# Selective scan stage: one activation table for Exp and Ln, the gate's Silu in four blocks between the last copies, first convolution products from two turned blocks

## The reference, cut to what matters

```
xz = x @ W_in;  xs, z = split(xz)
A = -(1..16)                                  # same for every channel
xs = silu(conv4(xs, conv_x_w) + conv_x_b)     # u
z  = silu(conv4(z, conv_z_w) + conv_z_b)      # the gate
dt_low, B, C = split(xs @ W_xdbl)             # 64, 16, 16
delta = softplus(dt_low @ W_dt + 2 * inv_dt)
for each token, for each state n of 16:
    h[n] = exp(-(n+1) * delta) * h[n] + delta * u * B[n]
    y += h[n] * C[n]
y = y + u * D
x = layernorm(x + concat(y, z) @ W_out + b_out)
```

## Time and profile before

| | us |
|---|---|
| median of 3 executions | 2578.47 |
| lowest, highest | 2573.18, 2580.49 |
| the profiled execution: its time | 2579.75 |
| its span (first to last instruction in the trace) | 2578.0 |
| the stage in question, from its first product to the last layer norm statistics | about 566.5 to 736 |
| PE, DVE, ACT, POOL busy over the whole span | 93%, 78%, 58%, 47% |

### The profile page before, as it was taken

The page is one execution under the profiler, slowest core; times in us unless marked ns, Lnnn a source line. Parts: engine busy times, 40 slices in busy tenths (PEclk is TensorE's granted clock), DMA queues, the critical chain, the costliest instruction groups (busy, mean ns, idle before and its releaser), DMA issues.

```text
span 2578.0 us, 41400 instructions
## 1 busy us (share of the span) xinstructions
PE 2385.0 (93%) x15006; PEld 1114.8 (43%) x15006; DVE 2009.2 (78%) x3088; ACT 1485.4 (58%) x2648; POOL 1202.6 (47%) x985
## 2 busy tenths in 40 slices
PE   6799997998969977997899999999999999999898
PEld 4444445452346754774333334333343334333345
DVE  7798886428979947875688897989888897989742
ACT  5586664637559946983555554555545554555462
POOL 2211112305847733762256665666656665666730
PEclk9799998999989999998999999999999999999999
DMA  5000001010000000000100000000000000000000
GB/s 218 1 1 1 1 1 59 1 70 1 0 17 2 2 1 1 2 2 17 46 5 10 10 6 9 10 10 6 9 9 10 10 6 9 10 10 9 6 1 17
DMA packets 21431, 39.37 MB, mean 15 GB/s; under 512 B 10542, under 2 KB 12718, under 8 KB 20332
## 3 DMA queue, kind: packets, MB, share of 16 engines
q1 hardware_dynamic: 21228, 36.73, 4.1%
HBM read 32.80 MB, written 2.35 MB: 14 GB/s over the span
## 4 chain that ended last, share of the span: by engine, by line
PE 76%; DVE 14%; ACT 4%; issue 4%; POOL 1%; DMA 0%; DVEq 0%; ACTq 0%; POOLq 0%; SPq 0%
PE PS L2978 16%; PE PS L2969 16%; PE PS L1393 6%; PE PS L2941 5%; PE PS L2151 2%; PE PS L2200 2%; PE PS L1375 2%; PE PS L814 2%; PE PS L815 2%; PE PS L816 2%; DVE NR L3189 1%; PE PS L2220 1%; PE PS L2924 1%; DVE WK L1925 1%; PE PS L2216 1%
## 5 line engine op out<-in xcount | busy, mean ns | idle before, releaser
L3088 ACT ACTIVATE WK<-PS 128x1024 f32<-128x1024 f32 x512 | 497.2, 1022 | 457.5 <-PE PS L2969 454.5
L3268 POOL TENSOR_TENSOR W<-W,WK 128x512 f32<-128x512 f32 x448 | 574.9, 1284 | 387.0 <-DVE W L3207 387.0
L3189 DVE TENSOR_REDUCE NR<-PS 128x2 f32<-128x1024 f32 x512 | 625.0, 1223 | 133.9 <-PE PS L2942 117.3
L2978 PE MATMUL PS<-WK,W 128*64 128x512 f32 x2048 | 494.1, 603 | 0.0
L2969 PE MATMUL PS<-WK 64*128 64x512 f16 (+1 forms) x4096 | 484.0, 376 | 0.6 <-issue 0.6
L3207 DVE TENSOR_TENSOR W<-W,WK 128x512 f32<-128x512 f32 x448 | 338.9, 759 | 9.1 <-ACT WK L3088 9.1
L2969 PEld LDWEIGHTS PS<-WK 64*128 64x128 f16 (+1 forms) x4096 | 199.0, 94 | 220.0 <-ACT WK L3088 6.5
L2978 PEld LDWEIGHTS PS<-WK,W 128*64 128x64 f32 x2048 | 124.0, 136 | 247.5 <-issue 170.0
L2941 PE MATMUL PS<-WK 64*128 64x512 f16 x512 | 195.4, 382 | 4.0 <-DVE NR L3189 3.5
L2942 PE MATMUL PS<-WK 64*128 64x512 f16 x512 | 195.4, 382 | 0.0
L2439 POOL TENSOR_TENSOR WK<-WK 128x768 f32<-128x768 f32 (+1 forms) x64 | 147.4, 2322 | 101.8 <-DVE WK L2364 101.8
(11 more groups left out here) (379 smaller groups left out, 4365.4 us busy)
## 6 DMA issues: line engine op xcount, KB each, us to landing
XB<-l_rdens SPq DMA_DIRECT2D x62, 128.0 KB, 2.9
W<-in_mw SPq DMA_DIRECT2D x8, 512.0 KB, 12.0
W<-in_l2w SPq DMA_DIRECT2D x1, 3114.0 KB, 11.6
W<-in_f1w SPq DMA_DIRECT2D x1, 2816.0 KB, 19.1
W<-in_l3w SPq DMA_DIRECT2D x1, 2816.0 KB, 9.9
W<-in_f3w SPq DMA_DIRECT2D x1, 2816.0 KB, 9.8
W<-in_mw SPq DMA_DIRECT2D x8, 256.0 KB, 12.4
W<-W SPq DMA_DIRECT2D x4, 384.0 KB, 3.7
```

The source lines that it names most:

```text
L2978: m = e.matmul(k.PS[64 * i:64 * i + 64, 4, :], self.V[:, kt, g, :], self.PTB[kt // 2 % 2][:, kt % 2, i, :], start=kt == 0, stop=kt == NT - 1)
L3088: e.activation(self.PTB[kt // 2 % 2][:, kt % 2, :, :], self.k.PS[:, 2 * (kt % 2):2 * (kt % 2) + 2, :], ACT.Exp, scale=1.0 / 64).then_inc(s ...
L3189: e.tensor_reduce(self.PM[ji % 2][:, u // 4, :, u % 4], self.k.PS[:, bk:bk + 2, :], AX.X, ALU.max).then_inc(self.maxes.sem)
L3268: e.tensor_tensor(ac, ac, p, ALU.add).then_inc(self.acc1.sem)
```

## The change

- **Table sets.** ACT loads LOGS by hand ahead of the first Abs, and once more ahead of the loop. Exp is now done by blocks of 512 (`dexp` counts four), so the start runs Abs, Exp, Ln of block 0 and then of block 1, and unit 10 does two Exps.
- **The gate's Silu** (`act_silu`, a block of 512 each) stands ahead of each of the last four `copy_c` (units 30 and 31); `zs` counts four. `pe_out` waits for its own block, and writes to banks 7, 1, 2, 3 (`YBANK`) instead of 0 to 3.
- **Output products of block 0** move into the loop, in unit 31 between the two `rows_c`.
- **End of DVE**: layer norm of block 0, then `dve_y` of blocks 2 and 3, then the other three.
- **Start of PE**: the convolution of block 0 waits for turned blocks 0 and 1 only, that of block 1 for 0 to 2. On DVE the copy of block 0 goes between the inverses of the norm and the scaling of the last rows.
- **DVE** does `delta` and `delta_u` of block 0, then of block 1.

```
@@ LayerNorm @@
     def dve_scale(self, e):
+        self.dve_inverses(e)
+        self.dve_scale_last(e)
+
+    def dve_inverses(self, e):
...
-        self.dve_rows(e, 4 * a, NT)
+
+    def dve_scale_last(self, e):
+        self.dve_rows(e, 4 * self.early, NT)
@@ Mamba.pe @@
         self.xt.pe(e)
+        e.wait_ge(*self.folded(2))
+        self.xt.ready(e, 1)
+        self.pe_conv(e, 0)
+        self.xt.ready(e, 2)
+        self.pe_conv(e, 1)
         self.xt.ready(e, 3)
-        e.wait_ge(*self.folded(2))
-        self.pe_conv(e, 0)
-        self.pe_conv(e, 1)
...
             self.rows_c(e, u, 0)
+            if u == 31:
+                e.wait_ge(*self.ld.wout(16))
+                self.pe_out(e, 0)
...
-        e.wait_ge(*self.ld.wout(16))
-        e.wait_ge(*self.zs(1))
-        self.pe_out(e, 0)
         self.pe_out(e, 1)
@@ Mamba.pe_out @@
         e.wait_ge(*self.y(b + 1))
-        if b < 2:
-            e.wait_ge(*self.inp(63 + b))
-        else:
+        e.wait_ge(*self.zs(b + 1))
+        if b == 1:
+            e.wait_ge(*self.inp(64))
+        elif b > 1:
             e.wait_ge(*self.scan(32))
@@ Mamba.act @@
-        self.act_abs(e, 0)
-        self.act_abs(e, 1)
-        self.act_exp(e, 0)
-        self.act_ln(e, 0)
-        self.act_ln(e, 1)
+        e.preload_act_table_set(LOGS)
+        for b in range(2):
+            self.act_abs(e, b)
+            self.act_exp(e, b)
+            self.act_ln(e, b)
...
         self.act_u(e, 3)
+        e.preload_act_table_set(LOGS)
         for u in range(self.UNITS):
+            if u >= 30:
+                self.act_silu(e, 2 * u - 60)
             self.copy_c(e, u, 0)
+            if u >= 30:
+                self.act_silu(e, 2 * u - 59)
             self.copy_c(e, u, 1)
...
-                self.act_exp(e, 1)
+                self.act_exp(e, 2)
+                self.act_exp(e, 3)
...
-        e.wait_ge(*self.zraw(4))
-        e.activation(self.ZS, self.ZS, ACT.Silu, bias=c("czb")).then_inc(self.zs.sem)
         e.preload_act_table_set(LOGS)
@@ new @@
+    def act_silu(self, e, b):
+        s_ = slice(b * 512, (b + 1) * 512)
+        e.wait_ge(*self.zraw(b + 1))
+        e.activation(self.ZS[:, s_], self.ZS[:, s_], ACT.Silu, bias=self.k.c("czb")).then_inc(self.zs.sem)
@@ Mamba.dve @@
-        self.before.dve_scale(e)
+        self.before.dve_inverses(e)
         self.begin.wait(e)
-        self.xt.dve(e)
+        self.xt.dve_block(e, 0)
+        self.before.dve_scale_last(e)
+        self.xt.dve_block(e, 2)
...
         for b in range(2):
             self.delta(e, b)
-        for b in range(2):
             self.delta_u(e, b)
...
         for b in range(NB):
-            if b == 2:
+            e.wait_ge(*self.out(b + 1))
+            self.ln.dve(e, b, four(PS[:, self.YBANK[b], :]))
+            if not b:
                 self.dve_y(e, 2)
                 self.dve_y(e, 3)
-            e.wait_ge(*self.out(b + 1))
-            self.ln.dve(e, b, four(PS[:, b, :]))
```

19 lines of the change are left out of this document (10 added, 9 removed).

## The result

The changed kernel takes 2568.59 us (median of 19 runs, 2564.57 to 2574.74), the kernel before on the same chip 2580.49 us (19 runs, 2572.88 to 2586.00); the ratio is 0.9961 with a 95% interval of 0.9949 to 0.9973, so the change saves 0.4%, clear of noise. In a second series the changed kernel took 0.9953 of the time (0.9935 to 0.9971). The forecast was 2568.8 us. The profiled execution took 2564.57 us (span 2562.8, mean granted clock 0.974), that of before 2579.75.

What follows compares the result with a forecast made beforehand. DVE paces the steady loop, so the saving comes from its idle places: 0.6 (start through unit 3) + 3.2 (units 12 to 16) + 5.9 (end) = 9.7 us, from 2578.47 to 2568.8 us; range 2564.0 to 2574.5.

Steps and rivals of the forecast that it cites:

- Start: Up to the first scan: PE's rows of B are the bound; gain 1.0 us, of which 0.3 from ACT.
- Unit 3: DVE's stall for a row of B at unit 3: gain between 0.1 and 2.0 us, taken 0.6.
- Units 12 to 16: Both DVE stalls go without the two loads, POOL is late next: 15.8 us instead of 18.92, gain taken 3.2.
- three units of 0.2 + 2.5 + 1.26 = 4.0 each: POOL in units 12 to 16: its time per unit with the added delta work, putting the last delta_u at 14.8 to 14.9.
- End: After the last scan: early Silu and load, output products in the loop and norms filling DVE's wait gain 5.9 us.
- less than 0.2: Unit 31: ACT's last copy ends at 720.0, POOL is busy until 720.2, so the work put into the loop costs nothing.
- Rival 1: End gives less, PE at the lower clock during block 0's products: gain there 4.4, total 8.2, 2570.3 us; chance 0.16.
- The drain: About 1380 ns with every switch of set; would make the end's gain about 4.7 and the whole 8.5 us.
- Rivals 2: Middle stays bound by POOL and PE's order, only 1.57 goes: gain 8.1, 2570.4 us; chance 0.16 alone or with Rival 1.
- rival 3: Slower: PE's clock does not come back after its wait for the first copy of C; 2587.4 us; chance 0.03.
- a clock under 0.9 past unit 4: Sign that would show the forecast wrong: granted PE clock below 0.9 after unit 4.
- The later stages: Behind the changed stage: their being longer than before was a sign of being wrong, which no term foresaw.

Runs made afterwards that it cites:

- u4_silu_behind: Changed kernel with block 0's output products behind the loop and the four Silus with their load behind the last copies of C; last scan to last add 15.83 us against 11.67.
- m1_out0_twice: Changed kernel with the eight output products of block 0 done twice in the loop; last scan to last add 13.46 us against 11.67.

## Why the prediction was right, and where it was not

The forecast of the time held nearly to the tenth, but not by its own sum: two errors cancelled. The stage gave 11.93 and not 9.7, and the median of before, 2578.47 in three runs, is 2580.49 in nineteen. With the right base and my sum it would have been 2570.8, with my base and the right sum 2566.5; with both, 2580.49 - 11.93, it is 2568.56. That this meets the measured 2568.59 so closely is chance as well: 11.93 comes from one execution of each kernel, and the changed kernel's second profile has the stage 3.46 longer.

**Start.** Forecast 1.0, measured 1.21. The mechanism is as told: DVE ready first, PE's rows of B the bound. The first product of the convolution came 0.89 earlier instead of 0.7. With the start undone 0.98 are lost, with the tables undone 0.57; they sum to more than 1.21 because each alone leaves the other as the bound (0.64 and 0.23 are what one alone gives against before).

**Unit 3.** Taken 0.6, range 0.1 to 2.0, measured 2.16: the most mis-sized term, and above its own range because the first scan gave 1.21 and not 1.0. The step that failed is "PE, at the lower clock twice as slow ... ends the first add_up at 597.0, a row and the second add_up at 599.1". In the frame of before, the clock was back at 597.0 (595.00 + 1.97), and the second pair took 1.03. I took the length of the low spell from the row of before, where it was 6.8 us, as if the length were a property of the place. The runs show two lengths, and at this place a restart of PE 0.5 to 1 us later goes with the longer one. The prices at the low clock were also a little small: "an add_up 1.7, a row of C 0.4", where the rows have 1.91 and 0.61. "With the clock back early it is DVE's own pace" was the right branch, and I put my value near the other.

**Units 12 to 16.** Forecast 15.8, bound by POOL; measured 15.05, DVE's pace. The step that failed is the sum of POOL's unit: "three units of 0.2 + 2.5 + 1.26 = 4.0 each". They stand 3.80 apart, because consecutive rows overlap by some 0.04, three times a unit, and the 4.0 is rounded up from 3.96; and POOL's first delta began 1.23 behind scan 12, not 1.5. (The gain "taken 3.2" is also 0.1 over the text's own 18.92 - 15.8.) The last delta_u ended 13.88 behind scan 12 instead of 14.8, in time for DVE. That POOL is next stands: in the runs with the longer low spell at unit 3, or a further one behind it, scan 12 to scan 16 took 15.13 to 15.55, and in u4_silu_behind the row of DVE's wait names POOL.

**End.** Forecast 5.9, measured 5.91, and the order of events is the one foreseen. By runs, the Silus' place is 3.72, DVE's order 0.52, the products' place 0.44; the remaining 1.2 is in no single undoing, since the run with Silus and products both put back still has Silus by blocks and DVE's new order. The margin of "less than 0.2" in front of POOL was real: eight more products made POOL wait 1.65. But POOL is not what bounds the end; m1_out0_twice shows PE busy without a break and the end later by just what PE has more to do, where the text asked only who waits for the copy. Rival 1 (low clock in the loop's last units) did not come in any of the profiles with the Silus in the loop; PE's waits for copies shortly before were not twice 1.2 but once 0.81 (row 706.94 of the changed kernel's trace).

**The drain** that the Trainium skill (ScalarE: Activation LUTs, "What ACT_TABLE_LOAD costs") adds to every switch of set would, by the prediction's estimate, have made the end 4.7: the load at 704.39 ends at 705.67 and Silu starts at 705.68, and the end gave 5.91. The measurement decides against it here.

**Rivals 2 and 3** did not occur. But rival 3's mechanism, a wait of PE from which the clock takes long to return, is what made the difference at unit 3 between 2.2 and 0; it cost one to two microseconds there and not eighteen. The prediction named a clock under 0.9 past unit 4 as a sign of being wrong. It occurs (0.66 in 611 to 616, behind PE's wait of 2.42 for DVE in unit 5) and costs nothing: DVE has no wait behind it, and before has the same 0.66 in 616 to 621. The later stages, on which I had put a condition, are 1.28 shorter in the profile after, with the same kernel text; over the 14 profiles the part behind the last add varies by 4 us.

## What to carry to other kernels

Where PE stands idle in a stage that another engine paces, ask for the time at which it resumes and not only for how long it waits: here a microsecond there came back as two at the next place where that engine is late. A chain that you add up for an engine with consecutive instructions should use the distance between two starts in the trace, not the sum of durations. And when a microsecond is to be judged in a kernel whose runs lie ten apart, measure stage intervals from an event ahead of the change: they repeat to 0.02 us unless the clock falls, and the row shows when it does.

## What the runs showed of the hardware

Three things that I had not expected. The granted clock can fall in the same place of the same program in one execution and not in another: in 2 of 14 profiles the convolution's first half ran partly at the lower level (8.57 and 9.84 us instead of 7.03 to 7.11), and both programs have another profile in which it did not. At the wait for the first copy of C the clock fell in 13 of 14 profiles; the lower level lasted until 28.7 to 29.2 us behind A where PE resumed by 25.5, and until 32.1 to 33.2 where it resumed at 25.9 or later, but behind the next long wait both lengths came with the same time of resumption. And filling the first wait with small products did not prevent the fall in one run of two.
